# Closing matrix products of a graph layer split into halves of 64 rows and 64 columns

## What is computed

```python
for t in range(ET):                       # 3 edge types
    Ve = jnp.einsum('ehd,dk->ehk', Vs, Wm[t])      # 8 heads, 32 x 32 matrices
    w = jax.nn.softmax(scores, axis=0)             # over all edges of the type
    msgs = msgs + jnp.where(mask[:, None, None], w[..., None] * Ve, 0.0)
agg = jax.ops.segment_sum(msgs.reshape(-1, OUT_DIM), tgt, num_segments=n)
```

## Time and profile before

| what | us |
|---|---|
| median of 3 runs | 1071.82 (1071.51 to 1072.44) |
| the profiled execution, its time | 1069.83 |
| the profiled execution, its span | 1068.1 |
| PE busy in the span | 880.7 |
| DVE, ACT, POOL busy | 806.2, 588.5, 638.9 |
| closing products L2191, first start to last end | 811.03 to 856.99 |

### The profile page before, as it was taken

How to read it: one execution, slowest core, us unless ns; L and a number is a source line. 1 busy time by engine, 2 the same in 40 slices (tenths; PEclk the granted TensorE clock), 3 DMA queues, 4 the chain that set the end, 5 groups by cost and what they waited for, 6 DMA issues and landing times. The chain is left out here.

```text
span 1068.1 us, 18060 instructions
## 1 busy us (share of the span) xinstructions
PE 880.7 (82%) x5049; PEld 634.7 (59%) x5049; DVE 806.2 (75%) x1708; ACT 588.5 (55%) x1532; POOL 638.9 (60%) x818
## 2 busy tenths in 40 slices
PE   5999999999657877777777777778777948999998
PEld 3776877877434444444444444444447937888886
DVE  6754788888568889898888898988866837886541
ACT  2655999997346666666666666666641213223220
POOL 4615777878677777777777777777720047672000
PEclk9999999999958788888878888887868969999999
DMA  9722344444588888888888888888826332110020
GB/s 284 252 82 90 135 163 146 144 146 153 170 262 252 249 247 250 246 250 254 246 248 254 248 249 252 249 248 252 254 69 242 107 115 70 50 48 4 1 94 27
DMA packets 111497, 189.61 MB, mean 178 GB/s; under 512 B 17861, under 2 KB 80140, under 8 KB 111396
## 3 DMA queue, kind: packets, MB, share of 16 engines
q0 software_dynamic: 38896, 129.86, 39.2%
q1 hardware_dynamic: 69220, 55.29, 16.8%
q10 hardware_dynamic: 3280, 3.28, 0.9%
HBM read 154.21 MB, written 34.16 MB: 176 GB/s over the span
## 5 line engine op out<-in xcount | busy, mean ns | idle before, releaser
L1406 POOL DMA_INDIRECT big<-kv_scratch,src_i x336 | 318.7, 949 | 102.1 <-issue 100.3
L1563 PE MATMUL ps<-edge 64*128 64x256 f32 x784 | 151.3, 519 | 16.2 <-DMA edge<-q_scratch 12.8
L1579 PE MATMUL ps<-big,edge 128*64 128x256 f32 x672 | 118.3, 484 | 37.2 <-DVE big L1748 21.1
L1689 DVE TENSOR_TENSOR big<-big,ps 128x1024 f32<-128x1024 f32 x84 | 102.4, 1219 | 41.0 <-DMA big<-kv_scratch,src_i 37.2
L1563 PEld LDWEIGHTS ps<-edge 64*128 64x128 f32 x784 | 89.5, 246 | 58.2 <-issue 47.7
L1579 PEld LDWEIGHTS ps<-big,edge 128*64 128x64 f32 x672 | 52.7, 167 | 85.5 <-DVE big L1748 43.1
L1477 ACT ACTIVATE edge<-edge 128x64 f32<-128x64 f32 x392 | 102.9, 334 | 0.0
L1696 DVE TENSOR_REDUCE ps<-big 128x32 f32<-128x1024 f32 x84 | 102.5, 1220 | 0.1
L1748 DVE TENSOR_TENSOR big<-big,ps 128x1024 f32<-128x1024 f32 x84 | 99.1, 1213 | 0.0
L2160 ACT ACTIVATE big<-ps,fb 128x256 f32<-128x256 f32 (+2 forms) x104 | 39.5, 462 | 101.9 <-PE ps L2226 101.9
L2226 PE MATMUL ps<-big 128*128 128x256 f32 (+2 forms) x416 | 91.0, 376 | 2.7 <-ACT big L2147 2.7
(11 more groups left out here) (353 smaller groups left out, 1895.8 us busy)
## 6 DMA issues: line engine op xcount, KB each, us to landing
edge<-q_scratch SPq DMA_DIRECT2D x196, 64.0 KB
edge<-key_scratch SPq DMA_DIRECT2D x98, 64.0 KB
big<-kv_scratch,src_i POOLq DMA_INDIRECT x336
agg_scratch<-big SPq DMA_DIRECT2D x16, 252.0 KB
xn_scratch<-big ACTq DMA_DIRECT2D x5, 640.0 KB, 6.6
mix_scratch<-big SPq DMA_DIRECT2D x25, 128.0 KB, 1.7
edge<-mix_scratch SPq DMA_DIRECT2D x1, 3200.0 KB, 12.7
big<-xn_scratch SPq DMA_DIRECT2D x25, 128.0 KB, 2.5
```

What stands on the lines that cost most here:

```text
L1406: pool.indirect_dma_start(kv_slots[s][:, k, :], None, kv_d[0:N, :], bass.IndirectOffsetOnAxis(ap=src_i[:, e:e + 1], axis=0)).then_inc(got[ ...
L1563: ins = pe.matmul(qr_ps[g % 2][:, (2 * hg + k) * D:(2 * hg + k + 1) * D], ohT[64 * hg:64 * hg + 64, g % 2, k * P:(k + 1) * P], qwin[64 * h ...
L1579: ins = pe.matmul(sums_of(g)[64 * hg:64 * hg + 64, :], oneh[:, s, k, hg * 64:hg * 64 + 64], kv_slots[s][:, 2 * hg + k, D:2 * D], start=(k ...
L1689: dve.tensor_tensor(k_rows, k_rows, qr_ps[g % 2].rearrange("p (k d) -> p k d", d=D), ALU.mult).then_inc(pr, 1)
```

## The change

Each product of 128 rows and 128 columns becomes two of 64 rows and 64 columns: features 0 to 63 against the upper left quarter of `bd_m`, and features 64 to 127 against the lower right quarter. The zero quarters are no longer multiplied. The two halves write to two neighbouring banks. A chunk now takes two banks, and there are three such buffers, banks 2 to 7, instead of four of one bank. The wait for a free buffer moves accordingly, and ScalarE's copy reads 2 x 128 columns out of two banks and puts them in the old order.

```diff
+        def chunk_ps(ck):
+            b = 2 + 2 * ((ck + 1) % 3)
+            return psum[:, b * 512:(b + 2) * 512].rearrange("p (h m) -> p h m", h=2)
...
-                    act.activation(keep[0:n, k % 2, ck % (UN // CG), :], ps[4 + ck % 4][0:n, 0:D], ACT.Copy).then_inc(ck_kept, 1)
+                    act.activation(keep[0:n, k % 2, ck % (UN // CG), :].rearrange("p (c h m) -> p h c m", c=C, h=2),
+                                   chunk_ps(ck)[0:n, :, 0:C * HP].rearrange("p h (c m) -> p h c m", c=C), ACT.Copy
+                                   ).then_inc(ck_kept, 1)
...
-                    at_least(pe, ck_kept, ck - 3)
+                    at_least(pe, ck_kept, ck - 2)
                     for ch, scaled in enumerate((sc_first, sc_second)):
                         pe.wait_ge(scaled, k + 1)
                         for t in range(ETY):
-                            ins = pe.matmul(ps[4 + ck % 4][0:n, ch * P:(ch + 1) * P], stg[k % 2][:, ch, t, at:at + n],
-                                            bd_m[:, t, :], start=(t == 0), stop=(t == ETY - 1))
+                            for hf in range(2):
+                                r = slice(hf * HP, (hf + 1) * HP)
+                                ins = pe.matmul(chunk_ps(ck)[0:n, hf, ch * HP:(ch + 1) * HP], stg[k % 2][r, ch, t, at:at + n],
+                                                bd_m[r, t, hf * HP:(hf + 1) * HP], start=(t == 0), stop=(t == ETY - 1))
```

## The result

The changed kernel takes **1107.96 us** (1106.19 to 1108.09, 4 runs) against 1071.66 us (1069.76 to 1072.44, 4 runs) of the kernel before: a ratio of 1.0344 (95% interval 1.0327 to 1.0361), 3.4% slower. The forecast was 1108.5, range 1098 to 1113.

A forecast was written before the change was run, and what follows sets the result against it. The prediction took TensorE's closing products (L2191, 45.96 us), paced by weight loads, as the bound. At 1.2 GHz 80.6, 1.7 and 0.5 make 82.8 us, so 1071.8 + 36.8 = 1108.6, rounded 1108.5; range 1098 to 1113.

The forecast's parts named there:

- The clock step: TensorE's closing products: half-empty 64-column intervals prevent the clock's rise at 814.4, leaving 1.2 GHz throughout; chance 0.76, +36.8 us.
- second rival: Closing products: issuing loads and short products is activity enough, so the clock rises at 814.4 as before.
- rivals 1 and 2: Closing products: clock rises at 814.4 and holds (1071.9 to 1073.1 us, 0.10) or falls at the store wait (1102.5, 0.05).
- Loads bind, and the loads of two halves overlap: Closing products: a pair of halves costs what one product did; at a given clock the gain is 0 to 1.2 us.
- The size: Stage of closing products at 1.2 GHz: 82.8 us against 45.96, +36.8 us.
- the pair at 1.2 GHz: Closing products: two halves replacing one product take 0.210 us, between bounds 0.206 and 0.217.
- Behind the stage: Joining products and feed-forward layer: early joining products stay hidden; the L2226 clock rise may shift, 1.7 us either way.
- The buffers: Three instead of four: TensorE waits one chunk earlier; cost 0 at 1.2 GHz, +1.3 us if the clock rises.
- Copy and VectorE: ScalarE's rearranging copy stays at 0.38 us, cost 0; VectorE's scaling, 2.30 against 5.04 us a unit, stays hidden.
- Rival 2: Closing products: clock rises but falls at the store wait, about 822.0 to 823.7; +29.4 + 1.3, 1102.5 us, chance 0.05.
- Rivals 1, 3 and 4: Closing products: clock rises and holds, no change (0.10); VectorE bounds, 1066 us (0.05); halves' loads queue, 1191 (0.04 with mishaps).

The follow-up runs named there:

- wide128: Changed kernel, but each 64-row half streams all 128 columns and ScalarE copies each half separately; 1195.79 against 1190.86 us for the kernel before, ratio 1.002.
- ring3: Kernel before with three chunk buffers instead of four, products whole; ratio 1.0031 to the kernel before, stage of closing products 47.4 us.
- start4: Changed kernel with chunks 0 to 3 streaming 128 columns a half, 64 from then on; 1103.9 against 1070.9 us for the kernel before, ratio 1.0307.
- warm: Changed kernel with four extra, never-read products of 384 columns ahead of the first chunk; 1072.83 against 1070.9 us for the kernel before, ratio 1.0020.
- wide96: Changed kernel with 96 columns a half, 32 of them zeros; ratio 1.0027 to the kernel before, stage of closing products 47.7 us.
- wide96_late: Changed kernel with 96 columns a half and feed-forward weights loaded behind the third and sixth store; ratio 1.0010 to the kernel before.
- after_late: Changed kernel with only the feed-forward weight loads moved behind the third and sixth store; ratio 1.0306 to the kernel before, stage 83.9 us.
- cols_only: Changed kernel with 128 rows in each load, only the columns halved to 64; single run 1313.72 us, 123 above the kernel before on that chip.
- start4_late: Changed kernel with 128 columns a half in chunks 0 to 3 and feed-forward weights loaded behind later stores; 1068.33 to 1094.83 us, median 1084.14.
- before_late: Kernel before with only the feed-forward weight loads moved behind the third and sixth store; 1070.04 against 1070.9 us, ratio 0.9991.

## Why the prediction was right

- **The clock step** was the whole of it. What streamed before the rise was what counted: the clock rose under 128 columns (before, wide128, ring3, start4), under 384 (warm) and under 96 (wide96, wide96_late), and not under 64 (after, after_late, cols_only), although PE was busy throughout. One of the two stretches that the forecast rested this on does not bear it out. From 776.9 to 780.3 the single columns of L1597 fill only the first 0.4 us; from 777.31 on 256-column products ran, at the low clock just the same. So the step stood on 807.6 to 811.0 alone, where PE also had gaps, and 0.76 was a bet that the runs then bore out. The forecast's "second rival" in that place is rivals 1 and 2, which both begin with a rise at 814.4.
- **Loads bind, and the loads of two halves overlap**: shown by wide128, wide96 (same pace with 64, 96, 128 columns) and cols_only (twice the time without row halves). At a given clock the change is worth nothing: start4_late (64 columns from chunk 4 on) and before_late have stages of 45.4 and 45.3 us. So the 0 to 1.2 us that I allowed as a gain is 0; the pair at 2.4 GHz takes 0.110.
- **The size**: +36.8 forecast, +37.9 measured in the stage. The term that was off is the pair at 1.2 GHz, 0.210 taken, 0.2133 measured, within the bounds 0.206 and 0.217. 0.0033 x 12 x 32 is 1.3 us; the last chunk and the ends came out 0.2 shorter, which leaves the difference of 1.1. The low value has a cause in the forecast's own row: the loads of L2182 start 0.213 us apart except for one first step of 0.165, and dividing their whole length by 11 gave 0.209; the step from 128 to 126 columns, taken by proportion, is not there at all (0.213 for both). That the forecast time, 1108.5, lies within 0.6 us of 1107.96 is luck: the sum was 1.1 us short in the stage and 0.4 in its start, and the 2.0 us by which the median lay above the profiled execution before did not come back after (1107.96 against 1108.09).
- **Behind the stage** nothing moved: the clock rises 4.8 us after the first product of the feed-forward layer in both kernels, so the 1.7 us either way was not needed.
- **The buffers** cost 0 as they stand and 1.4 us at the high clock (1.3 forecast; ring3). In wide128 it was 3.7, since there the clock fell at the wait.
- **Copy and VectorE**: 0.384 us a copy as before, VectorE waits 42.2 us for PE. Both at nothing, as costed.
- **Rival 2**, a rise that is lost at the wait for the store, did not happen here but is real: start4 is that case, at +33 us where I had priced it at +30.7, with full columns in the first four chunks and a longer wait. Rivals 1, 3 and 4 are excluded by the granted clock, by the equal pace at 2.4 GHz, and by a chunk of 2.56 us.

No version here beats the kernel before by more than can be measured: before_late is the nearest, at 0.9991.

## What to carry to other kernels

Before taking columns out of a stream of TensorE, ask what its interval is bound by: here the weight loads set it, so fewer columns bought no time and only emptied the array, and the emptied stream stayed at the low clock. A busy PE in the profile says nothing on that; look at PEclk where the stream starts and at what came just before it last rose. Where a stream starts at the low clock, columns that compute only zeros can be worth having (wide128, 34 us in the stage). And a stream that holds the high clock but does not raise it must not wait long: 64 columns kept it over a wait of 0.6 us in warm and lost it for the rest of the stage at 3.5 us in start4.

## What the runs showed of the hardware that I had not expected

- One and the same stream ran at either clock. The 64-column halves ran at 2.4 GHz for 44 us in warm and at 1.2 GHz for 84 us in the changed kernel; what PE did before was the difference.
- The rise came 3.1 to 3.5 us after the first product where 128 columns streamed (before, wide128, ring3, start4) and 6.6 and 6.3 us after it with 96 (wide96, wide96_late).
- A load of 126 columns takes its place for 0.2133 us at 1.2 GHz and 0.110 at 2.4, the same as the interval of whole products of 128 columns. Loads of 84 columns stand 0.140 us apart at 1.2 GHz (cols_only, last chunk).
- The loads of the two row halves start 7 ns apart at 1.2 GHz (after) and 3 ns apart at 2.4 GHz (wide128).
- Moving two 1 MB loads behind the stores moved the late store from the first to a later one, rather than removing it: ACT's longest wait for a store is 4.64 us ending at 823.28 before, and 2.76 us ending at 837.34 in before_late.
